# Attention scores from seven block products, with the key sums on GpSimd and VectorE

## The reference

```python
q, k_new, v_new = xn @ wq.T, xn @ wk.T, xn @ wv.T          # xn = layernorm(x)
k = concatenate([ctx, k_new]); v = concatenate([ctx, v_new])  # 1024 keys
attn = softmax(q @ k.T / sqrt(512))
x = x + tanh(g_xattn) * (attn @ v) @ wo.T
hidden = relu((layernorm(x) @ sign(up).T) * up_scale)       # 2048 wide
x = x + tanh(g_ffn) * (hidden @ sign(down).T) * down_scale * output_scale
```

## Time and profile before

| | |
|---|---|
| median of three runs | 608.14 us |
| the profiled execution | 608.41 us |
| its span (first to last instruction) | 606.6 us |
| TensorE busy | 598.5 us, 99%, 2786 matmuls |
| VectorE, ScalarE, GpSimd busy | 298.5, 245.1, 126.5 us |

### The profile page before, as it was taken

How to read it: one execution, slowest core, us unless ns; L and a number is a source line. 1 busy time by engine, 2 the same in 40 slices (tenths; PEclk the granted TensorE clock), 3 DMA queues, 4 the chain that set the end, 5 groups by cost and what they waited for, 6 DMA issues and landing times.

```text
span 606.6 us, 6935 instructions
## 1 busy us (share of the span) xinstructions
PE 598.5 (99%) x2786; PEld 496.8 (82%) x2786; DVE 298.5 (49%) x439; ACT 245.1 (40%) x366; POOL 126.5 (21%) x116
## 2 busy tenths in 40 slices
PE   8999999999999999999999999999999999999997
PEld 7888888888888888888888888888887878888885
DVE  4335532225632225632226658665548844766664
ACT  3723321213321214321125655564658545645531
POOL 5760303000303000303000305224132003242002
PEclk9999999999999999999999999999999999999999
DMA  8751303000303000503012212112121212241011
GB/s 299 273 171 38 106 1 110 29 0 1 104 1 131 8 0 1 239 4 104 1 36 70 89 52 78 62 35 71 35 70 35 83 56 70 70 133 42 1 70 69
DMA packets 20096, 43.20 MB, mean 71 GB/s; under 512 B 4832, under 2 KB 4832, under 8 KB 19680
## 3 DMA queue, kind: packets, MB, share of 16 engines
q1 hardware_dynamic: 20064, 42.76, 20.6%
HBM read 36.45 MB, written 6.30 MB: 70 GB/s over the span
## 4 chain that ended last, share of the span: by engine, by line
PE 95%; DVE 2%; ACT 1%; DMA 1%; SPq 0%; issue 0%; ACTq 0%
PE proj L454 33%; PE score L454 22%; PE score L532 19%; PE turn L517 12%; PE proj L517 5%; PE turn L446 2%; PE score L669 2%; DMA rows<-in_x 1%; PE proj L500 1%; PE turn L500 1%; DVE four_x L991 0%; ACT four_x L748 0%; DVE rows L1335 0%; DVE scaled L1332 0%; DVE neg_max L1011 0%; ACT probs L760 0%
## 5 line engine op out<-in xcount | busy, mean ns | idle before, releaser
L532 PE MATMUL score<-down_signs,hid_split 128*128 128x512 f32 x512 | 133.8, 390 | 0.6 <-DVE normed L1245 0.5
L532 PEld LDWEIGHTS score<-down_signs,hid_split 128*128 128x128 f32 x512 | 95.8, 188 | 21.7 <-DVE hid_split L1212 0.9
L756 ACT ACTIVATE four_x<-proj 128x512 fp32r<-128x512 f32 x60 | 35.8, 599 | 163.3 <-PE proj L454 163.3
L454 PE MATMUL score<-four_x 128*128 128x512 f32 x384 | 89.9, 391 | 0.0
L454 PE MATMUL proj<-probsT,four_x 128*128 128x512 f32 x384 | 88.4, 390 | 0.0
L454 PEld LDWEIGHTS proj<-probsT,four_x 128*128 128x128 f32 x384 | 71.9, 188 | 14.8
L454 PEld LDWEIGHTS score<-four_x 128*128 128x128 f32 x384 | 71.5, 188 | 14.5
L454 PE MATMUL proj<-four_x,weights 128*128 128x512 f32 x336 | 76.8, 389 | 0.0
L454 PEld LDWEIGHTS proj<-four_x,weights 128*128 128x128 f32 x336 | 63.0, 188 | 13.0
L997 DVE TENSOR_TENSOR four_x<-proj,four_x 128x512 fp32r<-128x512 f32 x44 | 30.3, 691 | 87.9 <-ACT four_x L756 87.9
L382 POOL TENSOR_TENSOR four_x<-raw_ctx,four_x 128x2048 fp32r<-128x2048 f32 x8 | 36.9, 4610 | 116.5 <-ACT four_x L748 116.5
(11 more groups left out here) (102 smaller groups left out, 645.9 us busy)
## 6 DMA issues: line engine op xcount, KB each, us to landing
raw_w<-in_ffn_w SPq DMA_DIRECT2D x24, 512.0 KB, 3.3
raw_ctx<-in_ctx_turned SPq DMA_DIRECT2D x4, 1024.0 KB, 8.1
raw_ctx<-in_ctx SPq DMA_DIRECT2D x4, 1024.0 KB, 5.4
result<-rows SPq DMA_DIRECT2D x16, 256.0 KB, 2.1
rows<-in_x SPq DMA_DIRECT2D x3, 1024.0 KB, 5.5
turned_x<-in_x_turned SPq DMA_DIRECT2D x3, 1024.0 KB, 7.8
...
```

What stands on the lines that cost most here:

```text
L454: last = pe.matmul(bank, lhs(l), rhs(r), start=start and i == 0, stop=stop and i == 2)
L532: last = pe.matmul(wide(r), hid_split[:, n % HR, s, r * P:(r + 1) * P], down_signs[:, chunk_of(q), :], start=(q == 0 and s == HI), stop=(q ...
L756: act.activation(dst, proj_bank(n), ACT.Copy, scale=scale).then_inc(proj_hi, 1)
```

## The change

The scores of 512 queries by 1024 keys are computed as a product of four blocks by four (queries in halves of rows, keys in the old and the new side, the 512 features in two halves) by seven block products in place of eight (A11, A12, ... are blocks of the queries, B11, ... of the keys, S1 to S4 and T1 to T4 are their sums and differences). A block product is 2 tiles x 2 feature chunks x 3 passes = 12 matmuls of 512 columns.

For this, keys and queries are carried out of PSUM in full precision (`key_out`, `query_out`), the sums of blocks are formed (`t_sum` on VectorE in the first batch and on GpSimd in the others, `s_sum` on VectorE), and every operand is split again (`t_high`, `s_high`, `t_low`, `s_low`). Two products are copied out by ScalarE, five sums per pair of tiles are formed by VectorE (`sum_scores`) in `probs`, which now holds four tiles; maxima and exponentials read them from there. The transposes move into the value jobs, one in the middle and one at the end of each. raw_ctx moves to the place of turned_x, so that the transposed context of the next batch is loaded after `next_lo`. The statistics of the next rows are taken after the last transpose of the batch. Of the core of the diff:

```diff
+        SCORE_ORDER = (A11, S3, A12, S2, S1, A22, S4)
+        SCORE_RIGHT = {A11: B11, S3: T3, A12: B21, S2: T2, S1: T1, A22: T4, S4: B22}
+        TILE_ORDER = (2, 3, 0, 1)
+        OLD, NEW = 0, 1
+        TURN_ORDER = ((2, NEW), (2, OLD), (3, NEW), (3, OLD), (0, NEW), (1, NEW), (0, OLD), (1, OLD))
+        T_SUMS, T_HI, T_LO = (T1, T3, T2, T4), (T1, T3, T2, T4, B22), (T3, T1, T2, T4, B22)
+        S_SUMS, S_HI, S_LO = (S3, S2, S4, S1), (A11, S3, A12, S2, S4, S1), (A11, S3, A12, S2, S1, A22, S4)
...
+            def context_rows(b):
+                sp.wait_ge(ctx_ready, turned_split(b) + 1)
+                sp.wait_ge(t_sums, nth(T_SUMS, b, T4))
+                sp.dma_start(raw_ctx[:, :, :], ctx_v[b]).then_inc(ctx_in, 16)
             def next_rows(b):
-                sp.wait_ge(normed_done, RT)
-                if b == 1:
-                    sp.wait_ge(turned, RT)
-                else:
-                    sp.wait_ge(next_lo, b - 1)
+                sp.wait_ge(ctx_ready, values_split(b - 1) + 1)
                 sp.dma_start(turned_x[:, :, :], x_turned_v[b]).then_inc(turned_x_in, 16)
                 sp.wait_ge(rstd_done, b)
                 sp.wait_ge(means_out, b)
                 sp.dma_start(row_facts[b - 1].rearrange("s r p -> p s r"), mean_rstd[:, :, :],
                              allow_slow_non_contiguous=True).then_inc(facts_stored, 16)
                 sp.wait_ge(facts_stored, 16 * b)
+                sp.wait_ge(scored, product_scored(b - 1, S3, 1))
                 sp.dma_start(all_facts[:, :, :], row_facts[b - 1:b].rearrange("a s r p -> a s (r p)").broadcast_to(
                     [P, 2, ROWS])).then_inc(facts_in, 16)
...
+            for b in range(BATCH):
+                context_rows(b)
                 if b + 2 == BATCH:
                     sp.wait_ge(attended, 2 * RT)
                     sp.dma_start(rows_away, rows[:, 0:2 * RT, :]).then_inc(rows_spilled, 16)
-            sp.wait_ge(next_lo, BATCH - 1)
+                if b + 1 < BATCH:
+                    next_rows(b + 1)
+                    sp.wait_ge(next_lo, b + 1)
+                    sp.dma_start(raw_ctx[:, :, :], ctx_turned_v[b + 1]).then_inc(ctx_in, 16)
+            sp.wait_ge(scored, product_scored(BATCH - 1, S3, 1))
...
+            def t_sum(b, i):
+                b11, b21, b12, b22 = raw_ctx[:, TOP, :], raw_ctx[:, BOTTOM, :], raw_new[:, TOP, :], raw_new[:, BOTTOM, :]
+                t1, t2 = raw_t[:, t_place(T1), :], raw_t[:, t_place(T2), :]
+                plus, minus = {T1: (b12, b11), T3: (b22, b12), T2: (b22, t1), T4: (b21, t2)}[i]
+                if i == T1:
+                    pool.wait_ge(ctx_in, 16 * (turned_split(b) + 1))
+                    pool.wait_ge(raw_kq, kq_out(b, 1))
+                elif i == T3:
+                    pool.wait_ge(raw_kq, kq_out(b, 3))
+                else:
+                    pool.wait_ge(t_sums, nth(T_SUMS, b, T1 if i == T2 else T2))
+                pool.tensor_tensor(raw_t[:, t_place(i), :], plus, minus, ALU.subtract).then_inc(t_sums, 1)
...
+            def score_product(b, i, t):
+                for c in range(2):
+                    for k, (l, r) in enumerate(PASSES):
+                        last = pe.matmul(score_bank(i, t), q_left(i, l)[:, c, t * P:(t + 1) * P],
+                                         key_right(SCORE_RIGHT[i], r)[:, c, :],
+                                         start=i in (A11, S3, S2) and c == 0 and k == 0, stop=c == 1 and k == 2,
+                                         skip_group_check=True)
                 last.then_inc(scored, 1)
...
+            def scores(b):
+                pe.wait_ge(ctx_ready, turned_split(b) + 1)
+                pe.wait_ge(s_ready, nth(S_LO, b, A11))
+                for t in range(2):
+                    pe.wait_ge(raw_kq, kq_out(b, DC + 2 + t))
+                    score_product(b, A11, t)
+                pe.wait_ge(t_ready, nth(T_LO, b, T3))
+                pe.wait_ge(s_ready, nth(S_LO, b, S3))
+                pe.wait_ge(attended, RT * b)
+                for t in range(2):
+                    score_product(b, S3, t)
...
+                pe.wait_ge(t_ready, nth(T_LO, b, B22))
+                pe.wait_ge(s_ready, nth(S_LO, b, S4))
+                for t in range(2):
+                    pe.wait_ge(score_sums, score_sum(b, AT_C22, t))
+                    score_product(b, S4, t)
...
+            def v_jobs(b):
+                if b == 0:
+                    pe.wait_ge(w_ready, SPLIT[W_V] + DC)
+                for r in range(RT):
+                    if r < 2:
+                        pe.wait_ge(score_c11, 2 * b + r + 1)
+                    else:
+                        pe.wait_ge(proj_lo, values_out(b, r - 2))
+                    for i, (lhs, rhs) in enumerate(v_terms(r)):
+                        last = product(proj_bank(proj0(b) + r), lhs, rhs, i == 0, i == DC - 1)
+                        if i == 1:
+                            turn_probs(b, 2 * r)
+                    last.then_inc(proj_done, 1)
+                    turn_probs(b, 2 * r + 1)
...
+                scores(b)
+                v_jobs(b)
                 n = proj0(b)
...
-                pe.wait_ge(turn_lo, turn0(b) + 2 * RT)
+                pe.wait_ge(proj_lo, values_out(b, RT - 1))
+                pe.wait_ge(turn_lo, turn0(b) + 6)
                 for e in range(DC):
                     new, old = attn_terms(e)
-                    pe.wait_ge(proj_lo, n + 4 + e - 1)
+                    if e >= 1:
+                        pe.wait_ge(proj_lo, values_out(b, DC + e - 2))
                     for i, (lhs, rhs) in enumerate(new):
-                        if e == 0:
-                            pe.wait_ge(proj_lo, n + i + 1)
                         last = product(proj[:, e % 2, :], lhs, rhs, i == 0, False)
                     if last_batch and e == DC - 1:
                         last.then_inc(new_read, 1)
+                    if last_batch and e < 2:
+                        turn_two(RT * e)
                     if e == 0:
+                        pe.wait_ge(turn_lo, turn0(b) + 2 * RT)
...
+            def keys_and_queries(b, e):
+                if e < DC:
+                    key_out(b, e)
+                else:
+                    query_out(b, e - DC)
+                if e == 1:
+                    t_high(b, T1)
+                if e == DC:
+                    t_high(b, T3)
+                    t_high(b, T2)
+                if e == DC + 1:
+                    s_high(b, A11)
+                    s_high(b, S3)
+                    t_high(b, T4)
+                if e == DC + 2:
+                    t_high(b, B22)
+            def first_products_out(b):
+                s_high(b, A12)
+                s_high(b, S2)
+                for t in range(2):
+                    act.wait_ge(scored, product_scored(b, A11, t))
+                    act.activation(probs[:, t, 512:1024], proj[:, t, :], ACT.Copy).then_inc(score_p1, 1)
+                s_high(b, S4)
+                s_high(b, S1)
+                for t in range(2):
+                    act.wait_ge(scored, product_scored(b, A12, t))
+                    act.activation(probs[:, t, 0:512], proj[:, t, :], ACT.Copy).then_inc(score_c11, 1)
...
+                first_products_out(b)
+                act.wait_ge(scored, product_scored(b, A12, 1))
                 context_high(values_split(b))
+                exponentials(b, 2)
+                exponentials(b, 3)
+                probs_out(b, 0)
+                exponentials(b, 0)
                 proj_out(m, new_side[:, HI, 0, :])
+                probs_out(b, 1)
+                exponentials(b, 1)
+                probs_out(b, 2)
                 proj_out(m + 1, new_side[:, HI, 1, :])
-                probs_out(b, RT - 1)
+                probs_out(b, 3)
+                probs_out(b, 4)
+                proj_out(m + 2, new_side[:, HI, 2, :])
+                probs_out(b, 5)
+                probs_out(b, 6)
+                proj_out(m + 3, new_side[:, HI, 3, :])
+                probs_out(b, 7)
                 if last_batch:
+                    for n in range(4):
+                        take_signs(n)
+                    two_rows_out(0)
                     take_signs(4)
-                proj_out(m + 2, new_side[:, HI, 2, :])
-                if last_batch:
-                    two_rows_out(0)
-                proj_out(m + 3, new_side[:, HI, 3, :])
-                if last_batch:
+                    proj_out(m + 4, qT[:, HI, 0, :])
                     two_rows_out(2)
+                    right_high(0, B11)
                     take_signs(5)
-                    proj_out(m + 4, qT[:, HI, 0, :])
-                    act.wait_ge(ctx_ready, values_split(b) + 1)
...
+                queries(b)
+                sum_scores(b, AT_C22, 0)
+                sum_scores(b, AT_C22, 1)
+                sum_scores(b, AT_C21, 0)
+                maxima(b, 2)
+                sum_scores(b, AT_C21, 1)
+                sum_scores(b, AT_C12, 0)
```

(24 more changed lines are left out.)

392 lines of the change are left out of this document (246 added, 146 removed).

## The result

The changed kernel takes 666.8 us (median of four runs, 666.46 to 668.04), the kernel before in the same session 608.1 (607.65 to 608.43). The ratio is 1.097, with a 95% interval of 1.0951 to 1.0989: slower by 58.7 us. The prediction was 673.6 with a range of 650 to 692.

The account below looks back on a forecast made before the run. TensorE, busy 598.5 of 606.6 us, was taken as the bound, with every added wait paid in full. The terms -10.9 + 1.5 + 5.2 + 34.5 + 10.6 + 11 + 6 + 7.6 gave +65.5, hence 673.6 us, range 650 to 692.

Parts of the forecast that it names:

- Removed matmuls: Scores: 336 matmuls instead of 384, 48 saved at 0.227 us each, -10.9 us.
- Changes of kind: Value stage: eight groups of transposes a batch, not four, with about 0.12 us per change of kind; +1.5 us.
- End of the value stage: Start of attention output, four times: TensorE waits 1.3 us for the last value block's low part; +5.2 us.
- The facts: Attention block 3, three batches: TensorE waits 11.5 us each behind late statistics of the next rows, stored and reloaded; +34.5 us.
- The signs: Last batch's transposes: ScalarE takes four signs in a row, TensorE waits 8.4 us, then 2.2 at the fifth; +10.6 us.
- Operands of the first batch: First batch's queries and first product: ScalarE's high parts and VectorE's key sums delay TensorE; +11 us.
- the exclusion: VectorE with two SBUF inputs and GpSimd reading SBUF exclude each other; operand stage costs 18.2 us with it, 4.8 without.
- The other three batches: First product of each: operands late through GpSimd's key sums and contention, 2.0 us each; +6 us, between 0 and 12.
- The clock: TensorE runs at 1.2 GHz behind long waits: 3 x 2.4 us, and 0.4 for the last; +7.6 us.
- The rival with full clock: TensorE's clock stays up in the waits: 666 us; chance 0.10.
- The rival without exclusion: VectorE and GpSimd don't exclude each other, so operands cost 4.8 and 0: 661 us; chance 0.12.
- those with timely facts: Facts' store is quick, no wait at block 3: 639 us, or 632 without those gaps' lower clock; chance 0.05.

Follow-up runs that it names:

- the last kernel: Changed kernel with early statistics, spread signs, staged value wait, reordered operand splits, and GpSimd's context-values low part held until VectorE made S4's low part: 603.4 us.
- the staged values: Changed kernel, but attention output starts when three value blocks are split and waits for the fourth only ahead of matmuls reading it: 669.8 us.
- GpSimd waits: Changed kernel, but in the first batch GpSimd starts its context subtraction and later weights only after VectorE's four key sums: 671.7 us.
- the filler: Changed kernel with 84 unused matmuls of 256 columns ahead of attention block 3 in the first three batches: 660.2 us.

## Why the prediction was right

- **Removed matmuls**, -10.9: in the last kernel the third batch, in which no wait is shown, lasts from 214.16 to 302.52:

```profile
214.16 2.88 PE L583 MATMUL proj<-four_x 128*128 128x512 f32 x12
...
302.52 2.88 PE L583 MATMUL proj<-four_x 128*128 128x512 f32 x12
```

  That is 88.36 us, 2.3 less than the 90.68 of the earlier trace rows, where 12 matmuls are 2.7: the price was right, and short waits in the other batches keep the rest of the 10.9 from the total.
- **Changes of kind**, +1.5: an estimated 0.6. A group of four transposes takes 0.36 us (66.95 to 67.31) and the change behind it 0.11 (67.31 to 68.78 is 1.47 for six matmuls, 65.59 to 66.95 is 1.36), where eight took 0.79 and 0.10 to 0.14 before; the prediction counted the changes, but not that two groups of four are 0.07 us shorter than one of eight. In the changed kernel:

```profile
65.59 1.53 PE L543 MATMUL proj<-weights,four_x 128*128 128x512 f32 x6
66.95 0.60 PE L535 MATMUL turn<-ident,probs 128*128 128x128 f32 x4
67.31 1.63 PE L543 MATMUL proj<-weights,four_x 128*128 128x512 f32 x6
68.78 0.60 PE L535 MATMUL turn<-ident,probs 128*128 128x128 f32 x4
```

- **End of the value stage**, +5.2: measured 3.9 in brackets, and 4.8 by the starts (79.75 + 0.36 for the last four transposes, then 81.32: 1.21 us for 1.3). The mechanism and the size were right. What the prediction did not say is that three of the four are worth nothing by themselves, as the staged values showed.
- **The facts**, +34.5: measured 31.0, from 10.57, 10.52 and 9.90 for 11.5. The store was issued about 6.7 us behind the last value matmul (7.1 worked out) and took 10.5 us in the median for 10.9. Taking the statistics early gave all of it back. The ends that the prediction gave for this wait are 0.5 us too low by its own rule (a pair 2 us quicker gives 9.5, one 2.5 us slower 14.0); the forecast doesn't use them.
- **The signs**, +10.6: measured 7.5. The first wait was 7.50 for 8.4; the second, of 2.2 at the fifth transpose, did not come. By the windows TensorE ran at half clock behind the first, which took 3.0 us of it, so it came later to the second. Two of the runs bear this out, since the low clock ended earlier in them (TensorE busy at 0.50 for 2.8 us where GpSimd waits and 3.4 with the filler, against 5.96): there the second wait was 0.66 and 0.40 us, and the fifth transpose started 5.9 us behind the third in both. At full speed it would have been reached after 3.5. GpSimd waiting:

```profile
414.18 1.08 PE L642 MATMUL turn<-ident,normed 128*128 128x128 f32 x8 [0.66 <-DVE normed L1345]
```

  The slow work and the second wait cover each other, as the prediction had it; it only charged the wait and not the work. Signs and clock together were forecast at 11.0 us there and took 10.5.
- **Operands of the first batch**, +11: measured 8.9, in the shape worked out with the exclusion: one long wait at the fourth query job (5.59 for 6.1), short ones behind it. Without it I had 4.8.
- **The other three batches**, +6: measured 2.8. GpSimd's sums take 2.40 us, as estimated, and only the fourth, beside VectorE's low part of T3, takes 3.26; the pair of engines met less than I assumed.
- **The clock**, +7.6: 12.0 by the windows, the term that was mis-sized most. I left out the stretch behind the first batch's wait (2.5 us) and took 0.4 for the last one, 3.0 by the windows; the three behind the facts cost 6.5 for 7.2. That the first 23 matmuls of the program run at 1.2 GHz stays inferred from their pace, 0.22 us each against 0.13 for the same at 7.40 us: the profile grants 1.00 there, before and after.

The six terms between the matmuls and the clock were forecast at 68.8 us and measured 57.4, the clock was 4.4 above its term: 7.0 less in all, hence 666.8 and not 673.6. So part of the nearness is luck, two errors against each other. (57.4 is the 54.1 of the brackets and the 3.3 left.) The rival with full clock gave 666, the time that was measured, and that is luck too: the windows show 12.0 us lost to the clock, and the filler alone gave 6.6 back; other terms were smaller by as much. The rival without exclusion (661) is excluded by the rows at 27.11 and 32.20, those with timely facts by the waits. The facts are the step that the sign of the result hangs on: with them early and all the rest kept, it is still slower (628.9), and the remaining waits (signs, first batch, first products, the pair at S4) had to go as well to leave a gain of 4.7 us.

Two rules of the Trainium skill were at stake. On the exclusion ("SBUF — State Buffer", "Who interferes with whom"), this case agrees: 128x512 took 4.72 and 4.69 us started 0.4 us behind GpSimd, 0.68 started ahead of it. The same section says that a VectorE instruction with at most one input in SBUF does not contend. The score sum at 138.58 (one input in PSUM) agrees: beside GpSimd's 4.62 us it took 0.69. On the clock the section "HAM oscillation — how this bites in real kernels" of the Trainium skill's "TensorE: Matmul & The Clock Gate" says that after a long wait for data TensorE starts again at the lower clock, and counts the loss from that beside the wait itself. The windows agree: 0.50 was granted in and behind every wait of 3.5 us and more that the runs show.
